# Expert tiles in pairs: the turn of h and the down-projection's turn over row groups

## The reference

```python
def expert_fn(Ug_e, Cg_e, Uu_e, Cu_e, Ud_e, Cd_e, w_e, rg, ru):
    g = jax.nn.silu(rg @ Ug_e.T @ Cg_e.T)
    u = ru @ Uu_e.T @ Cu_e.T
    rd = g * u @ Rd.T
    return w_e[:, None] * (rd @ Ud_e.T @ Cd_e.T)
```

## Time and profile before

| | us |
|---|---|
| median of three runs (867.01 to 867.39) | 867.18 |
| profiled execution, its own time | 868.9 |
| its span in the trace | 867.2 |
| stage B, first T to last D | about 399.7 to 739.4 |
| PE busy in the span | 779.4 |

### The profile page before, as it was taken

The page is one execution under the profiler, slowest core; times in us unless marked ns, Lnnn a source line. Parts: engine busy times, 40 slices in busy tenths (PEclk is TensorE's granted clock), DMA queues, the critical chain, the costliest instruction groups (busy, mean ns, idle before and its releaser), DMA issues.

```text
span 867.2 us, 22217 instructions
## 1 busy us (share of the span) xinstructions
PE 779.4 (90%) x6030; PEld 640.5 (74%) x6031; DVE 592.3 (68%) x2018; ACT 470.7 (54%) x1410; POOL 487.0 (56%) x692
## 2 busy tenths in 40 slices
PE   4899999999999999734999999999999999999995
PEld 2566666666666666523998998999899898888894
DVE  2578888888888888651565666666566566477886
ACT  2678888888888888622444444444444443233331
POOL 0126666666666666563555555555555556666766
PEclk9999999999999999955999999999999999999998
DMA  6345555555555555846644444444344443577885
GB/s 198 99 121 171 170 169 169 169 169 169 169 169 169 170 172 159 261 169 196 192 131 129 123 130 127 121 133 128 121 129 132 121 128 102 182 250 242 261 254 175
DMA packets 101890, 142.02 MB, mean 164 GB/s; under 512 B 16171, under 2 KB 83043, under 8 KB 101219
## 3 DMA queue, kind: packets, MB, share of 16 engines
q1 hardware_dynamic: 87523, 101.71, 39.7%
q0 software_dynamic: 14336, 39.94, 13.0%
HBM read 86.73 MB, written 58.82 MB: 168 GB/s over the span
## 4 chain that ended last, share of the span: by engine, by line
PE 40%; DMA 5%; issue 3%; DVE 3%; POOL 2%; SPq 1%; POOLq 0%; DVEq 0%; ACT 0%
PE bank L1196 9%; PE bank L1204 8%; PE bank L1218 6%; PE bank L1220 6%; PE bank L1211 4%; PE bank L1229 4%; DMA got<-yt_d 3%; DVE acc L1394 2%; DMA x2t<-xn2t_d 1%; PE bank L1267 1%; PE bank L1247 1%; POOL scaled L1330 1%; PE bank L1258 1%; PE bank L1254 1%; DMA xg<-xs_d 1%
## 5 line engine op out<-in xcount | busy, mean ns | idle before, releaser
L1319 POOL DMA_INDIRECT yt_d<-yo,name_i x160 | 158.0, 988 | 29.2 <-issue 20.2
L723 POOL DMA_INDIRECT xs_d<-rgu,sloti x128 | 127.5, 996 | 41.5 <-issue 31.9
L1364 DVE TENSOR_TENSOR h<-bank,gated 128x176 f32<-128x176 f32 x160 | 54.6, 341 | 90.9 <-ACT gated L1282 90.9
L1196 PE MATMUL bank<-down_w,rdt 128*128 x320 | 97.6, 387 | 18.4 <-issue 17.3
L1204 PEld LDWEIGHTS bank<-ht,rd_w 88*128 88x128 f32 x640 | 97.0, 192 | 8.4 <-issue 0.3
L1278 ACT ACTIVATE rdt<-bank 128x128 f32<-128x128 f32 x160 | 44.4, 278 | 103.4 <-PE bank L1204 103.4
L1282 ACT ACTIVATE gated<-bank 128x176 f32<-128x176 f32 x160 | 50.8, 318 | 89.2 <-PE bank L1220 88.6
L1204 PE MATMUL bank<-ht,rd_w 88*128 88x128 f32 x640 | 98.0, 275 | 0.0
L1317 POOL TENSOR_TENSOR fence<-ones 128x1 f32<-128x1 f32 x160 | 29.7, 185 | 120.2 <-DVE name_i L1354 119.9
L1353 DVE COPY yo<-bank 128x256 f32<-128x256 f32 x160 | 67.3, 420 | 24.5 <-PE bank L1196 24.5
L1359 DVE COPY ht<-bank 88x256 f32<-88x256 f32 x160 | 67.3, 421 | 22.5 <-PE bank L1211 13.4
(11 more groups left out here) (163 smaller groups left out, 1930.2 us busy)
## 6 DMA issues: line engine op xcount, KB each, us to landing
xg<-xs_d SPq DMA_DIRECT2D x160, 128.5 KB, 2.1
got<-yt_d SPq DMA_DIRECT2D x32, 512.0 KB, 4.2
raw<-in_raw SPq DMA_DIRECT2D x32, 496.0 KB
v<-v SPq DMA_DIRECT2D x128, 34.0 KB, 2.0
xs_d<-in_spare SPq DMA_DIRECT2D x4, 1028.0 KB, 7.0
xin<-in_x SPq DMA_DIRECT2D x32, 128.0 KB
ctxt<-in_ctxt SPq DMA_DIRECT2D x32, 128.0 KB
xres<-in_x SPq DMA_DIRECT2D x32, 128.0 KB
```

The lines of the kernel that those rows point to most:

```text
L723: nc.gpsimd.indirect_dma_start(xs_d, bass.IndirectOffsetOnAxis(sloti[:, b, k:k + 1], 0), rgu[:, b, k, :], None)\
L1196: nc.tensor.matmul(y_ps[b], rdt[:, b, :], weight(down_w, DOWN), start=True, stop=True)\
L1319: nc.gpsimd.indirect_dma_start(yt_d, bass.IndirectOffsetOnAxis(name_i[:, b, :], 0), yo[:, b, :], None)\
```

## The change

Tiles are taken two by two in R and H, in even steps only; D, U and T stay one a step. `h` of a pair lies side by side in one buffer (2 x 176 columns). H turns it in three pieces instead of four: 112 columns of the first tile (0 to 111), 112 of the second (its 64 to 175), and the 128 in the middle (the first tile's last 64 and the second's first 64), so that these last come out as rows 0 to 63 and 64 to 127 of one piece. R then is, for each tile, one product over 112 rows and one over 64 rows, where the two of 64 rows use different row groups of the array and different banks (6 and 7). The weights of R lie in the matching orders in `rd_a` (MOST = 112 rows) and `rd_b` (REST = 64 rows, twice), loaded by six DMAs in place of one. ACT and DVE copy once a pair. H has one bank instead of two, U waits for `h_done` and H for `ht_done` by name, the lags become 8, 10, 12 (LAG 13, LOOK 12), and so PE loads 15 expert numbers a round instead of 14.

```diff
-        rd_w = sb("rd_w", [HALF, 2, RANK])
+        rd_a = sb("rd_a", [MOST, 2, RANK])
+        rd_b = sb("rd_b", [P, RANK])
...
                         if at_step(s, 0):
                             constants(loads_then, ld_then)
+                            low, high = a["rd"][:, 0, :], a["rd"][:, 1, :]
+                            for rows, src in ((rd_a[0:HALF, 0, :], low), (rd_a[HALF:MOST, 0, :], high[0:MOST - HALF]),
+                                              (rd_a[0:HALF - REST, 1, :], low[REST:HALF]),
+                                              (rd_a[HALF - REST:MOST, 1, :], high), (rd_b[0:REST, :], high[HALF - REST:HALF]),
+                                              (rd_b[REST:P, :], low[0:REST])):
+                                sp.dma_start(rows, src).then_inc(ld_rd, 16)
...
-            TURN, UP, HTURN, RDOWN, DOWN, LAG = 3, 5, 7, 9, 11, 12
+            TURN, UP, HTURN, RDOWN, DOWN, LAG = 3, 5, 8, 10, 12, 13
...
-                        i, b = s - RDOWN, (ph - RDOWN) % 2
-                        if live(i, N):
-                            pe.wait_ge(ht_done, i + 1)
-                            if past(i, 1):
+                        i, b = s - RDOWN, (ph - RDOWN) // 2 % 2
+                        if (ph - RDOWN) % 2 == 0 and live(i, N):
+                            pe.wait_ge(ht_done, i + 2)
+                            if past(i, 2):
                                 pe.wait_ge(rdt_done, i)
-                            for c in range(2):
-                                m = nc.tensor.matmul(rd_ps, rd_w[:, c, :], ht[:, b, c, :],
-                                                     start=(c == 0), stop=(c == 1))
-                            m.then_inc(rd_psum, 1)
-                        i, b = s - HTURN, (ph - HTURN) % 2
-                        if live(i, N):
-                            pe.wait_ge(h_done, i + 1)
-                            for c in range(2):
-                                m = nc.tensor.transpose(ht_ps[b][:, c * P:(c + 1) * P],
-                                                        h[:, b, c * HALF:(c + 1) * HALF], ident[:, :])
-                            m.then_inc(ht_psum, 1)
+                            for t in range(2):
+                                nc.tensor.matmul(rd_ps[:, t, :], rd_a[:, t, :], ht[0:MOST, b, t, :], start=True, stop=False)
+                            for t in range(2):
+                                rows = slice(REST * t, REST * (t + 1))
+                                m = nc.tensor.matmul(rd_ps[:, t, :], rd_b[rows, :], ht[rows, b, 2, :],
+                                                     start=False, stop=True)
+                            m.then_inc(rd_psum, 2)
+                        i, b = s - HTURN, (ph - HTURN) // 2 % 2
+                        if (ph - HTURN) % 2 == 0 and live(i, N):
+                            pe.wait_ge(h_done, i + 2)
+                            if past(i, 2):
+                                pe.wait_ge(ht_done, i)
+                            for t in range(2):
+                                first = (INNER + REST) * t
+                                nc.tensor.transpose(ht_ps[0:MOST, t, :], h[:, b, first:first + MOST], ident[:, :])
+                            nc.tensor.transpose(ht_ps[:, 2, :], h[:, b, MOST:INNER + REST], ident[:, :])                                .then_inc(ht_psum, 2)
                         i, b = s - UP, (ph - UP) % 2
                         if live(i, N):
                             w = weight(up_w, UP)
                             pe.wait_ge(xgt_done, i + 1)
+                            if past(i, 2):
+                                pe.wait_ge(h_done, i - 1)
...
-                        i, b = s - RDOWN, (ph - RDOWN) % 2
-                        if live(i, N):
-                            act.wait_ge(rd_psum, i + 1)
-                            nc.scalar.activation(rdt[:, b, :], rd_ps, ACT.Copy).then_inc(rdt_done, 1)
+                        i, b = s - RDOWN, (ph - RDOWN) // 2 % 2
+                        if (ph - RDOWN) % 2 == 0 and live(i, N):
+                            act.wait_ge(rd_psum, i + 2)
+                            nc.scalar.activation(rdt[:, b, :, :], rd_ps, ACT.Copy).then_inc(rdt_done, 2)
...
-                            nc.vector.tensor_copy(ht[:, b, :, :].rearrange("p c t -> p (c t)"), ht_ps[b])\
-                                .then_inc(ht_done, 1)
+                            nc.vector.tensor_copy(ht[:, b, :, :], ht_ps).then_inc(ht_done, 2)
```

More of the change, by code:

```diff
@@ L42 @@
 HALF = INNER // 2
+REST = 64
+MOST = INNER - REST
 SHARED = 2 * INNER
@@ L147, in build @@
         bank03 = ps("bank03", [P, 4, 512])
-        bank4, bank5, bank6, bank7 = (ps(f"bank{k}", [P, 512]) for k in range(4, 8))
+        bank4, bank5 = (ps(f"bank{k}", [P, 512]) for k in range(4, 6))
+        bank67 = ps("bank67", [P, 2, 512])
+        bank6, bank7 = bank67[:, 0, :], bank67[:, 1, :]
         loads_first = [(ident, "ident"), (wq, "wq"), (bq, "bq")]
@@ L154, in build @@
         loads_then = [(wo, "wo"), (bo, "bo"), (rgu_w, "rgu"), (eiota, "eiota"), (tri, "tri"),
-                      (ebase, "ebase"), (names, "names"), (rd_w, "rd")]
-        LOOK = 11
+                      (ebase, "ebase"), (names, "names")]
+        LOOK = 12
         GROUP = 4
@@ L263, in build @@
             halves_done = asem("halves_done")
+            ld_rd = asem("ld_rd")
             sh_psum = asem("sh_psum")
@@ L384, in _ @@
                     sp.wait_ge(st_fill, 16 * 4)
+                    sp.wait_ge(ld_rd, 16 * 6)
                     sp.wait_ge(ld_shared, 4 * 16)
@@ L1057, in build @@
             gated = esb("gated", [P, 2, INNER])
-            h = esb("h", [P, 2, INNER])
-            ht = esb("ht", [HALF, 2, 2, P])
-            rdt = esb("rdt", [P, 2, P])
+            h = esb("h", [P, 2, 2 * INNER])
+            ht = esb("ht", [P, 2, 3, P])
+            rdt = esb("rdt", [P, 2, 2, P])
             yo = esb("yo", [P, RING, DIM])
@@ L1065, in build @@
             xgt_ps = bank03[:, 0, 0:2 * P]
-            ht_ps = [bank03[0:HALF, 1, 0:2 * P], bank7[0:HALF, 0:2 * P]]
+            ht_ps = bank03[:, 1, 0:3 * P].rearrange("p (c m) -> p c m", c=3)
             gu_ps = [bank03[:, 2 + k, 0:2 * INNER] for k in range(2)]
             y_ps = [bank4[:, 0:DIM], bank5[:, 0:DIM]]
-            rd_ps = bank6[:, 0:P]
+            rd_ps = bank67[:, :, 0:P]
             ld_xg = [esem(f"ld_xg{k}") for k in range(AHEAD)]
@@ L1195, in expert @@
                                 pe.wait_ge(yo_done, 2 * (i - 1))
-                            nc.tensor.matmul(y_ps[b], rdt[:, b, :], weight(down_w, DOWN), start=True, stop=True)\
+                            nc.tensor.matmul(y_ps[b], rdt[:, (ph - DOWN) // 2 % 2, b, :], weight(down_w, DOWN), start=True, stop=True)\
                                 .then_inc(ye_psum, 1)
-                        i, b = s - RDOWN, (ph - RDOWN) % 2
-                        if live(i, N):
-                            pe.wait_ge(ht_done, i + 1)
-                            if past(i, 1):
+                        i, b = s - RDOWN, (ph - RDOWN) // 2 % 2
@@ L1355, in expert @@
                                 .then_inc(yo_done, 1)
-                        i, b = s - HTURN, (ph - HTURN) % 2
-                        if live(i, N):
-                            dve.wait_ge(ht_psum, i + 1)
-                            nc.vector.tensor_copy(ht[:, b, :, :].rearrange("p c t -> p (c t)"), ht_ps[b])\
-                                .then_inc(ht_done, 1)
+                        i, b = s - HTURN, (ph - HTURN) // 2 % 2
+                        if (ph - HTURN) % 2 == 0 and live(i, N):
+                            dve.wait_ge(ht_psum, i + 2)
+                            nc.vector.tensor_copy(ht[:, b, :, :], ht_ps).then_inc(ht_done, 2)
                         i, b = s - UP, (ph - UP) % 2
@@ L1363, in expert @@
                             dve.wait_ge(gated_done, i + 1)
-                            nc.vector.tensor_tensor(h[:, b, :], gu_ps[b][:, INNER:2 * INNER], gated[:, b, :], ALU.mult)\
+                            k = INNER * ((ph - UP) % 2)
+                            nc.vector.tensor_tensor(h[:, (ph - UP) // 2 % 2, k:k + INNER], gu_ps[b][:, INNER:2 * INNER], gated[:, b, :], ALU.mult)\
                                 .then_inc(h_done, 1)
```

## The result

| | us |
|---|---|
| before, median of four runs beside it | 867.28 (867.01 to 867.59) |
| after, median of four runs | 888.62 (887.29 to 890.86) |
| ratio | 1.0244 (95% interval 1.0221 to 1.0268) |
| after, profiled execution / its span | 890.86 / 889.1 |

The account below looks back on a forecast made before the run. PE was taken to bound stage B, through its work per tile and a pause every eight tiles. Loop 15.5 + before step 16 0 + tail 0.5 + stage A 1.1 = 17.1 us, on 867.18: 884.3 us, range 871 to 890.

Parts of the forecast that it names:

- The price of a change of split: Stage B, into R's row halves and back for H: switches and exposed weight loads cost 0.38 us a pair, bounds 0 and 0.38.
- rival 3: R's two row halves run one after the other, each pair 0.22 us longer: 900 us; chance 0.07.
- The pause: PE's idle time once in eight tiles of stage B grows behind a light last step; round 0.86 us longer.
- issue pieces: Chain pieces called "issue" before a round's first down product: near 1.7 us instead of 0.97; staying at 1 would refute the forecast.
- the turn's load: Exposed weight load of H's first pass (112 columns) after the change back from row halves: 0.09 us a pair.
- rival 2: The idle time between rounds depends only on the end of PE's work: 872.2 us; chance 0.10.
- The loop's term: Stage B's 18 rounds (steps 16 to 159), each 0.86 us longer: 15.5 us.
- The tail: Behind the loop, R of the last pair comes after step 168's index load, one more down product follows: +0.5 us (0 to 1.5).
- Stage A: Five more loads issued in step 0 delay the second tile's xin: +1.1 us (0 to 2.4).
- Ramp: Stage B before step 16: about 0.8 us gained, 0.7 lost at step 16; set to 0 (-0.8 to +0.9).
- Waits: New waits ahead of U and H, for results two steps old, hold nothing up; T in the odd step is nearest to biting.
- rival 4: The turn of x in the odd step finds its copy late, each pair slips 0.2 us more: 899 us; chance 0.03.

Follow-up runs that it names:

- pairs alone: Kernel before with R and H of two tiles in even steps but R and H in their old pieces, no row groups: 885.91 us, ratio 1.0196.
- whole array: Changed kernel with R's two 64-row products run over all 128 rows, weights padded with zeros: 874.54 us, ratio 1.0085.
- T in two banks: Kernel before with two banks for the turn of x and one for H, so that turn waits for the copy two tiles back: 865.90 us, ratio 0.9976.
- late loads: R's six weight loads issued in step 2 of stage A: changed kernel 889.70 us; zero-padded kernel with two banks for the turn of x 853.06 us.
- the shift: Rounds starting at an odd step, lead of 19 entries, on the zero-padded kernel with two banks for the turn of x: 849.86 us, ratio 0.9767.
- misaligned: Kernel before with a table lead of 12 entries in place of 11, so PE's index load starts at 8k+1: 942.96 us, ratio 1.0864.

## Why the prediction was right, and where it was not

The forecast was 884.3 us in a range of 871 to 890, slower with a chance of 0.88. It came out at 888.6, 4.3 us above. On the profiled execution the sum's 17.1 us stand against 21.95.

- **The price of a change of split: right for the first change.** From the last pass over 112 rows to the first over 64 it is 0.205 us from start to start (forecast 0.20 instead of 0.11), the two halves start 7 ns apart, and the exposed load is 0.10 us (373 ns against 272). The second two passes follow 0.21 us after the first two: this load and one stride of 0.11. So the halves did run side by side, and rival 3 is out. Back to H it is 0.202 us, but the exposed load only 0.05 (the 320 of L1230's row below against 272), not the 0.09 that I had put there. The page has 146 ns for the weight load of a turn (L1249) and 192 for that of a product (L1217): I had priced the one like the other. The lengths of the two lines' passes in stage B follow (ns: minimum, median, maximum; half of L1220's are 373 and half 272, so the median is no pass's own):

```profile
L1220 PE MATMUL bank<-ht,rd_b x244: 272/322/373, 434.0 to 696.8; 64*128 64x128 f32 x122
...
L1230 PE MATMUL bank<-ident,h x122: 272/320/324, 434.4 to 697.2; 128*112 128x128 f32 x122
```

So the even step is 2.59 and not 2.62, 4 x 0.03 = 0.12 us a round. One reading of the prediction was off without harm: L514's two passes, given as a source of the stride of 0.11 us, start 0.14 apart (0.41 - 0.27); the 0.11 is that of stage B's turns. The "TensorEngine Tiling (Array Packing)" page of the Trainium skill says in its "Key Properties" that a change of tiling mode drains the engine; the 0.09 us of extra distance at either change agree. Its "Theoretical Speedup" gives up to 2x for a contraction of 64 rows. Here these four passes take 0.42 us to the next group's start, with a load and a change in them, against 0.45 on the whole array, and another 0.09 is paid on the way in.
- **The pause: right.** The issue pieces are 1.65 to 1.72 us (forecast 1.7; 0.97 before), the index load is 1.58 (1.59). ACT's copy for T ends at 706.46, and the sequencer's rows follow it as before:

```profile
L79 PEldq ALU_OP  x1: 32/32/32, 706.5 to 706.5; - x1
...
L174 PEldq TENSOR_LOAD <-table x1: 1580/1580/1580, 707.0 to 707.0; - x1
```

  The round grew by 0.75 us where 0.86 was forecast; the difference is the turn's load above. The run of pairs alone shows the mechanism without row groups, and rival 2 (the pause depends only on PE's end of work) falls with it: it would have had about 868 us. With T's wait taken away the same pairs fall to 858.6.
- **Not foreseen: the clock.** Three falls cost 5.1 us. This is the step that failed: I took the granted clock of before, 1.00, for the stage after as well, though the forecast itself nearly doubled PE's idle stretch. The loop's term came out as 13.3 + 5.1 = 18.4 in place of 15.5. Kernels with longer pauses have more falls (none of 18 at 0.66 to 1.17 us, 13 and 16 at 3.1 and 3.3), but at 1.9 us it was two or three and, over the whole array, none; what decides there is open.
- **The tail: too small.** Forecast +0.5 with a bound of 1.5, measured 1.15, and 1.3 more behind the last D, where I had none. Half of the latter can be read: the last tiles reach POOL faster than its 1.37 us a scatter, so its last seven follow one another without a gap (before, the last three), and the last starts 3.86 us after the last D instead of 3.19 (before: 742.11 and 738.92):

```profile
762.04 0.99 POOL L1339 DMA_INDIRECT yt_d<-yo,name_i  x1 [0.16 <-issue]
...
763.42 0.98 POOL L1339 DMA_INDIRECT yt_d<-yo,name_i  x1 [0.16 <-issue]
```

I had compared POOL's 1.3 us with the mean 2.2 us of a tile; in the tail the last three D start within 1.5 us (758.09 to 759.56). Both parts come with the pairing. From the D of step 160 to the last D it is 15.3 us before, 16.2 with pairs alone and 16.0 with the whole array; from the last D to the last scatter's start it is 3.2 us in the kernel before with T in one or in two banks, 4.0 with pairs alone and 3.9 with the whole array. The remaining 0.64 us do not: from the last scatter to the end it is 125.1 us before and 125.7 after, but 126.8 in the kernel before with T in two banks and 125.5 with pairs alone, so this is scatter between executions.
- **Stage A: right number, wrong reason.** The statistics landed at 16.37, as forecast (16.4), and stage B began 1.23 us later (forecast +1.1). But the runs with late loads and over the whole array show that stage B's start does not follow the statistics: it lies between 397.4 and 403.5 us in these kernels with no tie to the start. So the 1.2 us can't be put down to the late loads, and that they agree is luck. The term should have been 0 with a few us either way.
- **Ramp: right number, by luck. Waits: right.** From the first turn to the D of step 16 it is 0.11 us less (forecast 0). But this stretch takes 26.6 us after and 24.9 with late weights, which have the same stage B, and 22.7 to 28.2 in the other kernels whose rounds start at step 16 and whose load starts at 8k. T in the odd step was not late: rival 4 would have made each pair 0.2 us longer, and they take 2.59 and 1.25 us wherever the clock is at 1.00.

So the verdict came out by the mechanism that the forecast named, the longer pause at an unchanged length of the pair. That its centre is near owes something to luck: the falls of the clock left out (-5.1) and the tail (-2.0) were partly made up by the turn's load (+2.2), and the 1.1 us ahead of step 16 are small against the scatter there (its D lies between 420.9 and 426.9 us in the eight other kernels that start their rounds at it and load from 8k).

## What to carry to other kernels

Ask of a pause what the sequencer waits for, and how much work the engine still has at that point: a step made lighter in front of a loop's boundary can cost as much as a slower step elsewhere. A wait taken away counts only if no other wait keeps the sequencer as long, with what it has to dispatch behind it (1.4 us in one kernel, 27 in its paired form). Padding with zeros to the whole array can be cheaper than splitting it, when the split has to be entered and left around a few short passes; with more passes between the two changes it might pay, which no run here tried. The combination of the change's packing with the whole array and T in two banks gives 849.6 us (849.9 with the shift too), ratio 0.980 (0.975 to 0.985) to the kernel before, so about 2% faster.

## What the runs showed of the hardware

- The length of PE's index load depends on the entry at which it starts: 14 numbers take 1.52 us from entry 8k and 3.65 from 8k+1, in two kernels that differ in the lead of `table` alone; 15 numbers take 1.58 and 4.16. Why is open, and other starts than these two were not tried.
- From 8k the 15 numbers take 1.58 us where PE computes beside the load for 0.1 us, 1.92 to 1.99 where it does for 1.4 to 1.7, and 2.15 to 2.26 where it does for 2.0. That PE is the cause isn't shown: the other engines' work beside the load changes too, and 14 numbers with 0.8 to 0.95 us of PE beside them take only 1.52 and 1.47.
- SP's loads of four take 0.88 us in the kernel before, misaligned or not, and 1.27 us in the paired ones; why is open.
- Two products in the two row halves of the array start 7 ns apart and run side by side: the next two passes follow 0.21 us later, 0.10 of it the exposed load of the first and 0.11 one stride. In stage A four quarters of 256 columns start within 20 ns, and the next four 0.22 us later (0.27 after the first four), the stride of one such pass over the whole array.
- Around a change of split the distance of two starts is 0.09 us longer, when the rows alone change too (112 to 64 and back), and the first weight load behind it is exposed: 0.10 us for a product, 0.05 for a turn.
- On PE's sequencer a compare-and-branch of the loop takes 207 ns. The Trainium skill's "Advanced Engine Details and Errata" has about 108 ns under "Control Flow Timing"; the trace decides, for this engine and loop. On ACT it takes 45 ns in the same loop, on DVE 56.
- A fall of the granted clock from 1.00 to 0.50 costs 1.6 to 1.7 us each time it comes in this loop. It came in none of 18 rounds with pauses of up to 1.17 us, in none to three of 18 with 1.9 us, and in 13 and 16 with 3.1 and 3.3 us.
